# Audio tower on one core: shared weights in a buffer of their own, the first shared group joined to the attention drain, a reordered head, and unread TensorE products

## The reference

```python
win = xp[:, idx, :].reshape(B, num_slices, 8 * 80)          # 93 windows of 8 frames, stride 4
h = relu(win @ W1 + b1); h = relu(h @ W2 + b2)              # 640 -> 256 -> 256
h = (h - mean(h)) * rsqrt(var(h) + eps) * gamma + beta      # statistics over all clips and windows
h = h + attention(layernorm(h))                             # 16 heads of 64, per clip, 93 x 93
z = layernorm(h)
h = h + shared_expert(z) + sum_top2(gate * routed_expert(z)) + z   # 256 -> 1024 (gelu) -> 256, 8 routed
```

## Time and profile before

| what | value |
|---|---|
| median of 3 runs | 1072.42 us (1072.33 to 1073.98) |
| the profiled execution's own time | 1070.59 us |
| its span, first to last instruction | 1069.0 us |
| TensorE busy | 1018.5 us, 95% |
| granted clock, mean over the span | 0.985 |
| ends of tokenizer / attention / routed tiles | about 89, 610.5 and 980 us |

### The profile page before, as it was taken

One profiled execution on the slowest core, in us unless ns is written; L12 is line 12 of the kernel. 1 busy time (PEld: TensorE's weight loads), 2 busy tenths in 40 slices (PEclk: granted clock), 3 DMA queues, 4 the chain that ended last, 5 costly groups with the idle time before them and its releaser, 6 DMA issues. The chain is left out here.

```text
span 1069.0 us, 24219 instructions
## 1 busy us (share of the span) xinstructions
PE 1018.5 (95%) x8364; PEld 948.6 (89%) x8365; DVE 621.9 (58%) x1610; ACT 507.6 (47%) x1129; POOL 426.1 (40%) x535
## 2 busy tenths in 40 slices
PE   5995999999999999999999799999999999999998
PEld 5994798888888888888888699999999999999998
DVE  3665666767777676877757655433443343363565
ACT  3552554444544445454444464444555454454352
POOL 2001231445253443525343250606661626543885
PEclk9997999999999999999999699999999999999999
DMA  9615999900010100001011153331443134411555
GB/s 185 140 42 196 362 345 344 330 15 17 29 29 29 24 33 14 14 29 29 29 25 45 53 158 99 103 136 60 138 137 123 58 128 133 137 51 43 163 155 137
DMA packets 104628, 115.32 MB, mean 108 GB/s; under 512 B 29856, under 2 KB 94848, under 8 KB 104576
## 3 DMA queue, kind: packets, MB, share of 16 engines
q1 hardware_dynamic: 75936, 73.82, 22.6%
q0 software_dynamic: 18176, 29.12, 9.4%
q10 hardware_dynamic: 10464, 11.70, 3.3%
HBM read 51.53 MB, written 62.95 MB: 107 GB/s over the span
## 5 line engine op out<-in xcount | busy, mean ns | idle before, releaser
L1301 POOL TENSOR_TENSOR prob<-prob,rc 93x372 f32<-93x372 f32 x128 | 102.9, 804 | 294.4 <-DVE rc L1175 293.9
L1856 DVE TENSOR_TENSOR act_s<-up_ps,act_s 128x384 fp32r<-128x384 f32 (+1 forms) x168 | 81.7, 493 | 176.6 <-ACT up_ps L1703 175.3
L908 PE MATMUL pj_ps<-xg,wA 128*128 128x372 f32 x768 | 151.5, 344 | 5.4 <-DVE split L744 2.7
L1701 ACT ACTIVATE act_s<-up_ps 128x384 fp32r<-128x384 f32 (+1 forms) x168 | 73.7, 439 | 148.8 <-PE up_ps L1594 144.3
L908 PEld LDWEIGHTS pj_ps<-xg,wA 128*128 128x128 f32 x768 | 128.8, 190 | 13.3 <-DVE split L744 3.8
L894 PE MATMUL pj_ps<-wB,xg 128*93 128x512 f32 x384 | 102.6, 403 | 0.8 <-ACT h_s L666 0.8
L1069 ACT ACTIVATE probT<-t_ps 93x372 f32<-93x372 f32 x128 | 60.5, 473 | 83.7 <-PE t_ps L929 83.3
L1594 PE MATMUL up_ps<-rx,wB 128*128 128x256 f32 (+1 forms) x576 | 86.4, 308 | 0.7 <-issue 0.7
L1179 DVE TENSOR_TENSOR oT<-o_ps,oT 128x372 fp32r<-128x372 f32 x64 | 34.8, 543 | 89.3 <-ACT oT L1074 88.3
L1608 PE MATMUL dn_ps<-wB,act_s 128*128 128x256 f32 x720 | 85.5, 279 | 0.0
L1594 PEld LDWEIGHTS up_ps<-rx,wB 128*128 128x128 f32 x576 | 83.6, 188 | 1.6 <-issue 0.9
(11 more groups left out here) (201 smaller groups left out, 1958.7 us busy)
## 6 DMA issues: line engine op xcount, KB each, us to landing
slots<-zeros SPq DMA_DIRECT2D x8, 3072.0 KB, 23.3
y_rows<-zeros SPq DMA_DIRECT2D x5, 2688.0 KB, 20.0
rows_in<-slots SPq DMA_DIRECT2D x22, 384.0 KB, 3.5
y_rows<-rows_out ACTq DMA_DIRECT2D x22, 384.0 KB, 2.5
raw<-in_L_ffn_routed_up POOLq DMA_DIRECT2D x7, 1024.0 KB, 5.4
raw<-in_L_ffn_routed_down POOLq DMA_DIRECT2D x7, 1024.0 KB, 8.2
ln_out<-split SPq DMA_DIRECT2D x8, 744.0 KB
frames<-in_x SPq DMA_DIRECT2D x8, 400.0 KB
```

The costliest lines, as they stand in the source:

```text
L908: ins = pe.matmul(pj_ps[:, t, 0:N], wA[:, wp, at:at + P], xg[:, dp, m, :], start=(k == 0), stop=(k == 5))
L1301: pool.tensor_tensor(p, p, rc[:, u % 2, :].unsqueeze(2).broadcast_to([TP, 4, SL]), ALU.mult).then_inc(scaled, 1)
L1701: act.activation(act_s[:, HI, f, 0:width], up_ps[:, f % 4, 0:width], ACT.Gelu).then_inc(ract_hi, 1)
L1856: dve.tensor_tensor(act_s[:, LO, f, 0:width], up_ps[:, f % 4, 0:width], act_s[:, HI, f, 0:width], ALU.subtract).then_inc(ract_lo, 1)
```

## The change

It does these things:

- Head: VectorE clears the frames' padding and `grp0`, GpSimd only `grp1` after `ident`. The body loads of group 0 stay on SyncE, its three edge loads are issued by ScalarE, which then runs one small activation and loads the bias vectors. The first four turns go to four banks (`first_bank`). TensorE makes 32 unread transposes first. The second half of layer 1 of group 0 moves ahead of the last two turns of group 1. The loads of attention weights are issued one group later.
- TensorE makes 22 unread products after the last layer 2, and 15 and 3 (`spin`, 512 columns) in the attention's `start`.
- Shared weights get a buffer of their own, `wS`, which GpSimd fills from `raw2` in 16 parts during attention group 0. The splitting on ScalarE and VectorE in the last group, the ninth fetch and the wait of the fetch for expert 1 go. Even experts use wA, odd ones wB.
- Drain: the steps index to both, the ranks, pick and slots of group 6 move from steps 13 to 15 into the drain. Two of shared group 0's slices are computed before the attention block ends, into banks that `scores` used. ScalarE evaluates a gelu on one column there.
- Feed-forward, group 0: VectorE splits slices between the steps of the norm, and the order of tiles, down and routing is new.
- Layout: `wS`, `line_rest` (32 bytes) and `half_pair` (64 bytes) shift what lies behind; rows_in, rx, act_s and rows_out move ahead of the small tiles. `zeros` is halved. The starts modulo 128 are now: wS 0, sx 64, xg 0, oT 0, rx and act_s 64; in the tokenizer none moves.

```diff
+            def load_bodies(eng, g):
+                s = g % 2
+                for lo, hi in ((0, 80), (80, SL)):
+                    eng.dma_start(frames[lo:hi, s, :, 0:KF], slots_of(g, lo, hi)).then_inc(x_in[s], 16)
...
+            def load_edges(eng, g):
...
+            def first_bank(b):
+                if b < 2:
+                    return tr_ps[:, b, 0:3, 0:FG]
+                return l2_ps[:, b - 2, 0:3 * P].rearrange("p (q t) -> p q t", q=3)[:, :, 0:FG]
...
-                sp.wait_ge(pads, 1)
-                load_frames(0)
+                sp.wait_ge(edge_pad, 1)
+                load_bodies(sp, 0)
...
                 load_frames(1)
                 load_attn(0)
-                load_attn(1)
                 for g in range(2, NG):
                     sp.wait_ge(turned, GB * (g - 1))
                     load_frames(g)
-                    load_attn(g)
+                    load_attn(g - 1)
+                load_attn(NG - 1)
...
-                pe.wait_ge(consts, 4)
+                pe.wait_ge(consts, 2)
+                for _ in range(32):
+                    pe.transpose(tr_ps[:, 1, 3, :], ident[:, :], ident[:, :])
                 for b in range(GB):
                     turn(0, b)
-                for g in range(NG):
+                layer1(0, 0)
+                turn(1, 0)
+                turn(1, 1)
+                layer1(0, 1)
+                turn(1, 2)
+                turn(1, 3)
+                for g in range(1, NG):
...
                 layer2_by_inputs(NG - 1)
+                for _ in range(22):
+                    pe.matmul(l1_ps[:, 0, 0:N1], w2[:, HI, 0, 0:P], t1s[:, HI, 0, :], start=True, stop=True)
...
+                act.wait_ge(edge_pad, 1)
+                load_edges(act, 0)
+                act.wait_ge(consts, 1)
+                act.activation(b1c[:, 0:1], zero_c[:, :], ACT.Copy).then_inc(warmed, 1)
+                act.wait_ge(warmed, 1)
                 for v, t in ((b1, b1c), (b2, b2c), (gamma, gam), (beta, bet)):
...
+                def spin(count):
+                    for _ in range(count):
+                        pe.matmul(y_ps[:, 0, :], wB[:, HI, 0:P], wA[:, HI, 0:512], start=True, stop=True)
                 def start():
                     rows_tile(pe, -1, 0, 0)
                     rows_tile(pe, -1, 1, 0)
+                    spin(15)
                     for c in range(C):
...
                     pe.wait_ge(tri_set, 2)
+                    spin(3)
                     qk_tile(-1, "q0")
...
                     values(g, NJ - 1)
+                    rank_tile(pe, g, g - 1)
                     output(g, NJ - 1)
+                    pe.wait_ge(sx_in, 16)
+                    pe.wait_ge(sh_lo, SH_PARTS)
+                    pe.wait_ge(shifted, NG * NU)
+                    for f in range(2):
+                        shared_up(pe, sc_ps[:, f, 0:N], f)
...
-                    shared_hi(3)
                     take_turned(g, NU - 1)
                     take_o(g, NJ - 1)
+                    act.activation(warm[:, :], zero_c[:, :], ACT.Gelu).then_inc(warmed, 1)
...
                     take_o(g, NJ - 2)
-                    shared_lo(2)
-                    shared_lo(3)
+                    for step in ("index", "expert", "masks", "both"):
+                        route(dve, g - 1, step)
                     take_o(g, NJ - 1)
+                    take_ranks(dve, g, g - 1)
+                    route(dve, g - 1, "pick")
+                    route(dve, g - 1, "slots")
                     add(g)
...
+                def shared_part(q, low):
+                    cols = slice(q * 512, (q + 1) * 512)
+                    if not low:
+                        pool.wait_ge(raw2_in, 32)
+                        pool.tensor_tensor(wS[:, HI, cols], raw2[:, cols], zero_c[:, 0:1].broadcast_to([P, 512]), ALU.add
+                                           ).then_inc(sh_hi, 1)
+                    else:
+                        pool.wait_ge(sh_hi, q + 1)
+                        pool.tensor_tensor(wS[:, LO, cols], raw2[:, cols], wS[:, HI, cols], ALU.subtract).then_inc(sh_lo, 1)
...
+                        if not behind:
+                            shared_part(*divmod(u, 2))
...
-                fetch(E, 0, sh_up[0].rearrange("(c p) n -> p c n", p=P), sh_down[0].rearrange("(c p) n -> p c n", p=P))
...
-                up(wA, 0, range(0, 5))
+                up(wS, 0, range(2, FC))
                 back_tile(pe, LG, 1, 1, LN, z_rows)
                 back_tile(pe, LG, 1, 0, LN, z_rows)
-                up(wA, 0, range(5, 7))
+                down(wS, 0, range(0, 1))
                 logits_tile(pe, LG, LN)
-                up(wA, 0, range(7, FC))
-                down(wA, 0, range(0, 1))
+                down(wS, 0, range(1, C))
                 rank_tile(pe, LG, LN)
-                down(wA, 0, range(1, C))
...
                 moments(dve, LG, 1, LN)
+                splits(0, range(0, 1))
                 spread(dve, 1, LN)
+                splits(0, range(1, 2))
                 fused_root(dve, 1, LN)
+                splits(0, range(2, 4))
                 normalise(dve, LG, 1, LN, z_rows)
-                splits(0, range(0, 4))
+                splits(0, range(4, 7))
                 lo(dve, LG, 1, 1, LN)
```

More of the change, by code:

```diff
@@ L377, in _ @@
                 act.wait_ge(vec_in, 64)
-                for g in range(NG):
+                relu1(0, 0)
+                turned_hi(1, 0)
+                turned_hi(1, 1)
+                relu1(0, 1)
+                turned_hi(1, 2)
+                turned_hi(1, 3)
+                attn_part(0)
+                for g in range(1, NG):
                     relu1(g, 0)
@@ L979, in group @@
                             v_tile(g, V[s])
-                        if s == NU - 1 and behind:
+                        if s == NU - 1 and behind and ahead:
                             rank_tile(pe, g, g - 1)
@@ L1179, in take_o, with routing @@
                     dve.tensor_tensor(oT[:, j % 2, LO, :], o_ps[:, 0:N], oT[:, j % 2, HI, :], ALU.subtract).then_inc(o_lo, 1)
-                def routing(s, place, n):
+                def routing(s, place, n, ahead):
+                    if not ahead and s > 12:
+                        return
                     plan = {11: ("max", "shift", ""), 12: ("sum", "recip", "scale top"), 13: ("", "", "index expert masks both"),
@@ L1195, in group @@
                             shift(g, s)
-                        if s == NU - 1 and behind:
+                        if s == NU - 1 and behind and ahead:
                             take_ranks(dve, g, g - 1)
                         if behind:
-                            routing(s, 0, g - 1)
+                            routing(s, 0, g - 1, ahead)
                         if s >= 1 and not early:
@@ L1629, in _ @@
                 turn_rows(0)
-                down(wA, 2, range(2, C))
+                down(wS, 2, range(2, C))
                 pe.wait_ge(x_lo, 1)
@@ L1819, in _ @@
                 route(dve, LN, "shift")
-                splits(0, range(5, 6))
-                for step in ("sum", "recip", "scale", "top"):
+                add(0, 0)
+                for step in ("sum", "recip", "scale", "top", "index", "expert", "masks", "both"):
                     route(dve, LN, step)
-                splits(0, range(6, 7))
-                for step in ("index", "expert", "masks", "both"):
-                    route(dve, LN, step)
-                splits(0, range(7, FC))
+                add(0, 1)
                 take_ranks(dve, LG, LN)
@@ L1829, in _ @@
                 route(dve, LN, "slots")
+                add(0, 2)
                 keep(dve, LN, z_rows)
-                for c in range(C):
-                    add(0, c)
                 splits(1)
```

163 lines of the change are left out of this document (84 added, 79 removed).

## The result

The changed kernel takes 1059.59 us (median of four, 1057.71 to 1060.51) where the kernel before took 1072.43 beside it: a ratio of 0.9874, 95% interval 0.9863 to 0.9886. Its profiled execution is the fastest of the four, 1057.7 us with a span of 1056.1. The forecast was 1057.

The account below looks back on a forecast made before the run. TensorE was taken as the bound, busy 95%, with gains only in idle time and low clock at three seams. 4.3 + 2.0 + 9.1 = 15.4 us off 1070.6, plus 1.8 to the median, gave 1057 us; range 1052 to 1066.

Parts of the forecast that it names:

- The lower end of the range: Whole kernel: 1052 us, said to be where the bounds of head and drain are both used by half.
- The seams: Three places with TensorE idle or at a low clock: head, tokenizer to attention, attention's drain with start of the feed-forward.
- Head: Program start up to layer1(1, 0): earlier frames, shorter chain and a raised clock gain 4.3 us, bounds 2 and 5.5.
- the 0.7 us for the frames: Head: VectorE clearing the padding and edge loads on ScalarE bring the first turns 0.7 us forward, bounds 0 and 1.5.
- The wait for group 1's frames: Head, after layer 1's first products: two turns need group 1's frames, put at 14 us, a new wait of about 0.8 us.
- The rule of the Trainium skill: Head: full clock does not engage in transpose mode, so 2.3 instead of 4.3 us; transposes or slices rival 0.15.
- Tokenizer to attention: Step between the two: unread products keep the clock up during the norm, gain 2.0 us, bounds -1.9 and +3.0.
- Drain and start of the feed-forward: Attention's end to up of group 1: removed parts and routing steps, slices ahead, higher clock; gain 9.1 us, bounds 3 and 12.
- What costs nothing: GpSimd's 16 parts taken as 0, bound +1; tile 0's rows and the end's gathers move along; ninth fetch, expert 1 wait bound 1 us.
- Layout: Moved xg and oT in the attention, 1728 products: taken as 0, bounds -2 to +7 us.
- that rival: Attention: equal offsets of both operands cost 13.5 us at 8 ns, giving 1070.6 us; slower from 17.5 us, chance 0.05.
- The first rival: Drain: the clock falls all the same, the chain to the block's end takes some 5 us more, 1062 us; chance 0.25.

## Why the prediction was right

**The sum.** 15.4 us were foretold against the profiled execution, 12.9 measured; against the medians 12.8. The 1057 lies 2.6 us below the median, inside the range. The seams gave 3.1 + 2.2 + 9.3 = 14.6 us, 14.7 with the 0.16 inside the attention; 1.8 of it went behind them, for which the sum had nothing. The 1.8 us added for the step from the profiled execution to the median came out as 1.9, in part by luck: in the changed kernel falls of the clock in some executions make much of this step, and the prediction had no such term. The lower end of the range is not what its sentence says: half of the bounds left in head and drain (1.2 and 2.9 us) would lead to 1055, all of them to 1053. Nothing hung on it.

**Head: 4.3 said, 3.1 measured, within its bounds.** The term that failed is the 0.7 us for the frames: they came 0.47 us later, 0.26 of it since VectorE begins its clearing later than GpSimd did and SyncE's first load waits for it. The edges on ScalarE, which I had bring part of it, bring nothing. Layer 1 started at 11.51 instead of 10.3, and from the first turn on the 3.0 us to it are those of the forecast. The wait for group 1's frames, which I had at 0.8 us, was none to 0.24. That the 32 transposes raise the clock was right in this kernel: 1.00 is recorded from 6.91 us, while they alone ran on TensorE, and from 15.2 us without them; layer1(1, 0) came 1.7 us later then. What I had not reckoned with is that the clock falls again behind them in four of ten profiles, so the 3.1 us are those of a good one. The rule of the Trainium skill that I set against it (TensorE: Matmul & The Clock Gate, PE-mode transpose) would by my reckoning have made 2.3 us of it. The trace does not agree: these transposes ended 109 ns apart where they began 213. It lists them as MATMUL, so whether they run in the mode that the page means, no run here shows.

**Tokenizer to attention: 2.0 said, 2.2 measured,** 1.90 of it given back when the fill was left out. The 18 products took 3.33 us (3.1 said); the 15 took 3.67 us (3.2 said) and ended before the norm did.

**Drain and start of the feed-forward: 9.1 said, 9.3 measured,** but with errors inside. By the forecast the turn stands at 596.3 and the last output at 602.1, less the 5.45 us that were gained before: 590.8 and 596.6, measured 590.79 and 596.57. Slice 6 waited 1.12 us, behind the third split after the root as said, not 1.7. What I had wrong is the weight of the parts of the change: I gave the slices 2 us of it, and as far as the runs tell they gain nothing by themselves; the order at the block's end trades a wait of 1.38 us for one of 1.12. The moved parts and the moved routing steps carry the seam. Put back alone they cost 5.6 and 5.9 us of its 9.4 (3.8 and 5.6 us of the whole), where the low parts are 4.8 us of VectorE's time and the four steps some 1.3: so they are not additive, and for the steps the clock is most of it.

**What costs nothing.** GpSimd's 16 parts took 1.04 and 1.28 us each beside 33.9 us of GpSimd's idle time in the first group, and TensorE sat idle 0.1 us before its turns there. The first product of q of group 1 came 53.34 us behind that of group 0, and 53.17 with the parts back on the other engines: 0.2 us at most. Rows of tile 0: 1.23 us of wait, moved along. The end: on the gathers, as said, but they were not only moved along: of 14.2 us that the last shared groups came sooner, 12.9 reached the end. Some 0.9 us went between the last store and the first gather and 0.5 us in the gathers.

**Layout: 0 said, 0 measured.** In the attention moving xg and oT by 64 bytes does nothing. The reason given, slices 1488 and 496 bytes apart that spread over many offsets, was not tested there, but the runs without pad bear it out: the shared groups read the same act_s in three chunks 496 bytes apart, and their down products of 256 columns went from a median of 118 ns to 120 in the first chunk, 119 in the second and 118 in the third. The price I had put on that rival is real elsewhere: the routed tiles read act_s in slices 1536 bytes apart, twelve times 128, all at one offset, and pay 6 ns a product when it is that of the weights. The pad kept that away, as it was kept away before the change.

**The first rival** is half true. No low stretch in the profile on record, but one in the same kernel's next profile, at 593.4 us. It cost 1.4 us, not the 5 that I gave it, because the stretch was 3.4 us long and not 17; it makes most of the 1.8 us by which that execution's span is the longer one. So the forecast of a drain at the higher clock throughout is right for most profiles, not for all.

## What to carry to other kernels

Fill for the clock is worth what the wait behind it leaves: put unread products (better: real ones that are due later) where the engine waits, but end them before what sets the block's end: 34 of them that overran it put the next products off by 1 us in the profile. Where a last phase runs dry, first look at which engine's postponable work stands ahead of its short steps: without the moved routing steps the profile had a stretch of 13.7 us at half the clock. And do not judge such a change by one profile, since the places of the falls differ between executions. And when operands' slices lie a multiple of 128 bytes apart, check that the weights and the activations do not share their place within 128 bytes: 64 bytes of pad were worth 7 us of 1060 here.

## What the runs showed that I had not expected

- Equal places within 128 bytes of the loaded and the streamed operand cost at 256 columns, where 113 to 119 ns become 120, and nothing at 384 (173 ns). Moving both by 64 bytes changes nothing, moving one takes it away.
- Where the clock falls to 0.50 differs between executions, with the same instructions at the place: in 4 of 10 profiles in the head at 11.0 to 12.4 us, in 4 of the 10 with an unchanged step into the attention at 88 to 90 us, in 2 of the 8 with an unchanged drain at 593 us. The two with more fill had none, which by these shares, taken as independent, two profiles would have by chance once in some fourteen times. What decides it in one execution was not found.
- A fall can be free: 15 products that took 5.25 instead of 3.67 us ended in time for VectorE's normalised rows, and the time to the first scores stayed at 78.8 us.
